# Half a buffer of x's statistics moved to VectorE, the first row's x and k split on VectorE, and the second row's q and k projected before the first row's maxima

## What is computed

```python
# per layer; g(x) is the group norm, C = 32, 8 heads
q = proj(Wq) * C ** -0.5; k = proj(Wk); v = proj(Wv)          # of g(x)
logits = einsum('abhqc,abhkc->abhqk', q, k) + bias (+ mask in layer 1)
weights = softmax(logits, axis=-1)
gate = sigmoid(g(x) @ Wg.T + gating_bias)
x = x + (gate * (weights @ v)) @ Wo.T + bo
```

## Time and profile before

| | us |
|---|---|
| median of 3 runs | 3541.76 (3537.06 to 3541.86) |
| the profiled execution | 3537.66 |
| its span, first to last instruction | 3535.9 |
| first product of the row loop, layer 0 | 111.71 |
| last output products of layer 0 | 1816.19 |
| mean granted TensorE clock | 0.991 |

### The profile page before, as it was taken

How to read it: one execution, slowest core, us unless ns; L and a number is a source line. 1 busy time by engine, 2 the same in 40 slices (tenths; PEclk the granted TensorE clock), 3 DMA queues, 4 the chain that set the end, 5 groups by cost and what they waited for, 6 DMA issues and landing times.

```text
span 3535.9 us, 122483 instructions
## 1 busy us (share of the span) xinstructions
PE 3378.7 (96%) x36216; PEld 2679.8 (76%) x36216; DVE 3392.7 (96%) x11676; ACT 2927.4 (83%) x5457; POOL 3010.4 (85%) x2066
## 2 busy tenths in 40 slices
PE   0799999999999999999979999999999999999997
PEld 0577887778877788777847777877788777887775
DVE  5799999999999999999959999999999999999997
ACT  4588988889888898888857888888888888888885
POOL 3388889888898889888948898898888989898896
PEclk9999999999999999999979999999999999999998
DMA  9555555555555555555545555555555555555552
GB/s 375 166 116 124 125 121 119 118 125 125 119 119 120 125 125 117 119 122 125 120 121 109 120 125 127 124 121 120 126 127 121 120 122 127 127 119 121 123 127 83
DMA packets 463461, 454.11 MB, mean 128 GB/s; under 512 B 55440, under 2 KB 453904, under 8 KB 462880
## 3 DMA queue, kind: packets, MB, share of 16 engines
q1 hardware_dynamic: 255584, 252.91, 29.2%
q10 hardware_dynamic: 207808, 200.33, 26.1%
HBM read 182.39 MB, written 67.24 MB: 71 GB/s over the span
## 4 chain that ended last, share of the span: by engine, by line
PE 93%; DMA 2%; DVE 2%; ACT 1%; SPq 1%; issue 1%; POOL 0%; ACTq 0%; DVEq 0%; POOLq 0%
PE proj_a L922 19%; PE proj_b L922 19%; PE av_bank L949 13%; PE max_bank L933 13%; PE exp_bank L938 12%; PE proj_a L978 10%; PE den_bank L960 6%; PE proj_b L970 1%; DMA probs<-in_xT 1%; DMA k_stack<-k_lo 1%; DVE probs L820 0%; DVE max_bank L808 0%; SPq L376 0%; SPq L306 0%; PE den_bank L908 0%
## 5 line engine op out<-in xcount | busy, mean ns | idle before, releaser
L808 DVE CUSTOM_DVE_ANT_0 max_bank<-max_bank,bias_q 128x256 f32<-128x256 f32 x4096 | 1621.0, 432 | 54.2 <-PE max_bank L933 44.9
L478 POOL TENSOR_TENSOR probs_sum<-probs 128x1024 f32<-128x1024 f32 x508 | 1205.6, 2373 | 356.4 <-ACT probs L519 167.0
L820 DVE TENSOR_TENSOR probs<-exp_bank,bias_k 128x512 f32<-128x512 f32 x2048 | 1378.8, 674 | 10.6 <-PE exp_bank L938 10.6
L933 PE MATMUL max_bank<-k_stack,q_stack 96*128 96x256 f16 (+1 forms) x4096 | 786.5, 273 | 11.5 <-DMA k_stack<-k_lo 8.5
L938 PE MATMUL exp_bank<-q_stack,k_stack 100*128 100x256 f16 x4096 | 784.2, 272 | 9.8 <-DVE probs L820 6.9
L516 ACT ACTIVATE probs<-probs,mask_bias 128x1024 f32<-128x1024 f32 x512 | 560.4, 1142 | 35.2 <-issue 28.4
L519 ACT ACTIVATE probs<-probs 128x1024 f32<-128x1024 f32 x512 | 512.4, 1048 | 39.8 <-issue 33.9
L808 DVE DVE_READ_ACCUMULATOR2_ANT row_max<- 128x1 f32 x4096 | 533.0, 130 | 0.0
L949 PE MATMUL av_bank<-probs,v_sb 128*32 128x256 f32 x8192 | 497.4, 383 | 1.0 <-ACT probs L516 0.6
L938 PEld LDWEIGHTS exp_bank<-q_stack,k_stack 100*128 100x128 f16 x4096 | 394.0, 97 | 74.6 <-DVE probs L820 13.9
L933 PEld LDWEIGHTS max_bank<-k_stack,q_stack 96*128 96x128 f16 (+1 forms) x4096 | 400.7, 99 | 60.8 <-DMA k_stack<-k_lo 9.2
(11 more groups left out here) (171 smaller groups left out, 7038.4 us busy)
## 6 DMA issues: line engine op xcount, KB each, us to landing
q_stack<-q_hi SPq DMA_DIRECT2D x512, 128.0 KB
k_stack<-k_hi SPq DMA_DIRECT2D x512, 128.0 KB
q_stack<-q_lo SPq DMA_DIRECT2D x256, 128.0 KB
k_stack<-k_lo SPq DMA_DIRECT2D x256, 128.0 KB
y<-in_xT ACTq DMA_DIRECT2D x128, 256.0 KB, 3.5
layer_out<-y ACTq DMA_DIRECT2D x128, 256.0 KB, 4.0
y<-layer_out ACTq DMA_DIRECT2D x128, 256.0 KB, 3.6
out<-y ACTq DMA_DIRECT2D x128, 256.0 KB, 3.6
```

Source lines behind the costliest of these rows:

```text
L478: pool.tensor_tensor(probs_sum[:, g], pr[:, :, 0, :], pr[:, :, 1, :], ALU.add).then_inc(sum_ready, 1)
L808: op = dve.tensor_tensor_reduce(out=max_bank[h % 2][:, t, :], in0=max_bank[h % 2][:, t, :], in1=bias_q[:, h, t, :], scale=1.0 / FINE, scal ...
L820: dve.tensor_tensor(probs[:, r.ring(2), h], exp_bank[h % 2][:, :, :], bias_k[:, h], ALU.add).then_inc(logits_ready, 1)
L933: op = pe.matmul(bank_[:, t, :], q[0:n, t * P:(t + 1) * P], k[0:n, :], start=True, stop=True)
```

## The change

Four things are changed.

1. **Statistics.** ScalarE takes only the first 512 tokens of buffer 0 in each turn, VectorE the other 512 of it (two more BN_STATS a turn) and buffers 1 to 3 as before. Buffer 0 is refilled when both have counted it off. `neg_start` comes from VectorE's half of buffer 0.
2. **First row of each layer.** A new function `first_row(l)` on VectorE, between `normalisation(l)` and its slots, makes x_norm, x_hi, x_lo, k_hi and k_lo of row 0. They leave ScalarE (x_norm, x_hi, k_hi, k_f32) and GpSimd (x_lo, k_lo). ScalarE keeps q_hi and q_f32, GpSimd q_lo. ScalarE's table for the exponential is loaded right behind the square root.
3. **Fillers.** In place of 20 behind the group averages and 20 at the end of slot 0: 4 before the first average, 2 between the two, 10 behind them, none in slot 0.
4. **Second row.** In slot 1 of each layer TensorE projects q and k of row 1 at the start, ahead of the first maxima products of row 0, with all waits of these projections; v and gate stay at steps 3 to 5.

The row loop from slot 2 on is unchanged on every engine.

```diff
@@ sync
             def stat_free(c, i):
                 if i == 0:
                     wait(sp, act_stat, 4 * c, sp_passed)
-                else:
-                    wait(sp, stat_used, 3 * c + (i - 3), sp_passed)
+                wait(sp, stat_used, 4 * c + (i - 3), sp_passed)
...
@@ gpsimd, slot
-                    low_half(s, 1)
+                    if not s.first():
+                        low_half(s, 1)
...
                 r = s.plus(1)
-                if r.active():
+                if r.active() and not r.first():
...
@@ scalar
-                    act.activation(out_, x_stat[0][:, ct], ACT.Identity if k < 2 else ACT.Square,
+                    act.activation(out_, x_stat[0][:, ct, 0:512], ACT.Identity if k < 2 else ACT.Square,
...
                 high_gated(s.plus(-5))
-                if s.active():
+                if s.active() and not s.first():
                     split_high(s, 1)
...
@@ vector, statistics
-                    for t in range(n):
-                        op = dve.bn_stats(stats[:, ct, bass.ds(c * (3 * n) + ((i - 1) * n + t), 1), :],
+                    for t in range(1 if i == 0 else 0, n):
+                        op = dve.bn_stats(stats[:, ct, bass.ds(c * STAT_PARTS + (i * n + t - 1), 1), :],
                                           x_stat[i][:, ct, t * 512:(t + 1) * 512])
...
             with dve.Fori(3, STAT_TURNS - 1) as c:
-                for i in range(1, STAT_BUFS):
+                for i in range(STAT_BUFS):
                     statistics(c, i)
...
+            def first_row(l):
+                r = Row(l, 0, 0)
+                i, k_scale = r.ring(2), 1.0 / W_SCALE
...
+                for c in range(CT):
+                    op = dve.tensor_scalar(x_norm[:, i, c], x_in[:, i, c], rstd[:, c:c + 1], shift_x[:, c:c + 1],
+                                           ALU.mult, ALU.add)
+                op.then_inc(x_norm_ready, 1)
...
+                dve.tensor_copy(x_hi[:, i], x_norm[:, i]).then_inc(x_hi_ready, 1)
+                dve.wait_ge(x_hi_ready, r.count(1, 1))
+                dve.tensor_tensor(x_lo[:, i], x_norm[:, i], x_hi[:, i], ALU.subtract).then_inc(x_lo_ready, 1)
+                dve.wait_ge(k_psum, r.count(1, 1))
+                dve.tensor_scalar(qk_hi[1][:, i], pb[:, :, :], k_scale, None, ALU.mult).then_inc(qk_hi_ready[1], 1)
+                dve.wait_ge(qk_hi_ready[1], r.count(1, 1))
+                dve.scalar_tensor_tensor(out=qk_lo[1][:, i], in0=pb[:, :, :], scalar=k_scale, in1=qk_hi[1][:, i],
+                                         op0=ALU.mult, op1=ALU.subtract).then_inc(qk_lo_ready[1], 1)
+                dve.wait_ge(qk_lo_ready[1], r.count(1, 1))
+                dve.sem_inc(qk_f32_ready[1], 1)
...
@@ tensor
+            def project_q(s):
+                wait(pe, v_ready, s.plus(-1).count(1, 1))
+                wait(pe, out_left, s.plus(-6).count(1, 1))
+                pe.wait_ge(x_hi_ready, s.count(1, 1))
+                project(s, 0, pa, 0, None)
+                project(s, 0, pa, 1, q_psum)
+
+            def project_k(s):
+                wait(pe, gate_ready, s.plus(-1).count(1, 1))
+                wait(pe, fine_ready, s.plus(-2).count(1, 1))
+                project(s, 1, pb, 0, None)
+                project(s, 1, pb, 1, k_psum)
+
             def slot(s):
+                second = isinstance(s.turns, int) and s.off == 1
+                if second:
+                    project_q(s)
+                    project_k(s)
...
-                    if step == 7 and isinstance(s.turns, int) and s.off == 0:
-                        keep_busy(20)
...
+                keep_busy(4)
                 pe.wait_ge(norm_v, 6 * l + 1)
                 pe.matmul(pa[:, 0, 0:CT], group_avg[:, :], mean_var[:, :, 0], start=True, stop=True).then_inc(norm_avg, 1)
+                keep_busy(2)
                 pe.wait_ge(norm_c, l + 1)
                 pe.matmul(pb[:, 0, 0:CT], group_avg[:, :], mean_var[:, :, 1], start=True, stop=True).then_inc(norm_avg, 1)
-                keep_busy(20)
+                keep_busy(10)
```

More of the change, by code:

```diff
@@ L76, in active, with first @@
         return not isinstance(self.turns, int) or 0 <= self.off < ROWS
+    def first(self):
+        return isinstance(self.turns, int) and self.off == 0
     def last(self):
@@ L345, in load_bias_k @@
                 else:
[L346 removed]
+                    sp.wait_ge(stat_used, STAT_LOADS)
                     sp.wait_ge(act_stat, 4 * STAT_TURNS)
@@ L567, in slot @@
                     act.dma_start(x_in[:, i], channel_major(src[l], r.index() * TOK, TOK)).then_inc(x_loaded[i], 16)
-                if s.active():
+                if s.active() and not s.first():
                     split_f32(s, 1)
                 r = s.plus(1)
-                if r.active():
+                if r.active() and not r.first():
                     i = r.ring(2)
-                    if r.off == 0 and isinstance(r.turns, int):
+                    if r.off == 1 and isinstance(r.turns, int):
                         act.wait_ge(norm_v, 6 * (l + 1))
@@ L620, in slot @@
                     act.activation(x_hi[:, i], x_norm[:, i], ACT.Copy).then_inc(x_hi_ready, 1)
-                    if r.off == 0 and isinstance(r.turns, int):
-                        act.preload_act_table_set("exp_and_others")
                 if s.active():
@@ L726, in _ @@
             with dve.Fori(3, STAT_TURNS - 1) as c:
-                for i in range(1, STAT_BUFS):
+                for i in range(STAT_BUFS):
                     statistics(c, i)
             c = STAT_TURNS - 1
+            statistics(c, 0)
             statistics(c, 1)
-            dve.wait_ge(stat_used, 3 * c)
-            aggregate(early_mv, 0, 3 * n * c).then_inc(mix, 1)
+            dve.wait_ge(stat_used, 4 * c)
+            aggregate(early_mv, 0, STAT_PARTS * c).then_inc(mix, 1)
             next(mixed)
             statistics(c, 2)
-            tokens = STAT_TURNS * STAT_TOK
+            tokens = STAT_TURNS * 512
             dve.wait_ge(act_stat, 4 * STAT_TURNS)
@@ L996, in slot @@
                         logits(r, h, False)
-                    if step == 1 and s.active():
-                        wait(pe, v_ready, s.plus(-1).count(1, 1))
-                        wait(pe, out_left, s.plus(-6).count(1, 1))
-                        pe.wait_ge(x_hi_ready, s.count(1, 1))
-                        project(s, 0, pa, 0, None)
-                        project(s, 0, pa, 1, q_psum)
-                    if step == 2 and s.active():
-                        wait(pe, gate_ready, s.plus(-1).count(1, 1))
-                        wait(pe, fine_ready, s.plus(-2).count(1, 1))
-                        project(s, 1, pb, 0, None)
-                        project(s, 1, pb, 1, k_psum)
+                    if step == 1 and s.active() and not second:
+                        project_q(s)
+                    if step == 2 and s.active() and not second:
+                        project_k(s)
                     if step == 3 and s.active():
```

38 lines of the change are left out of this document (26 added, 12 removed).

## The result

| | before | after |
|---|---|---|
| median of the runs side by side | 3540.45 (3536.5 to 3545.3, 8 runs) | 3527.68 (3524.64 to 3529.61, 8 runs) |
| the profiled execution | 3537.66 | 3529.61 |
| its span | 3535.9 | 3527.8 |

The ratio is 0.9968, with a 95% interval of 0.9959 to 0.9977: 11.3 us faster (8 to 14.5); the two medians are 12.8 us apart. The forecast was 3525.5 in a range of 3517 to 3535. The two profiled executions differ by 8.1 us only, because that of before was one of the shorter and that of after the longest of eight; hence the means over several profiles further down.

The account below looks back on a forecast made before the run. TensorE and VectorE were taken as 96% busy, leaving only each layer's fill to shorten. Terms 3.7 - 0.4 + 1.2 + 4.0 + 1.2 + 4.3 + 1.0 = 15.0 us, 14.5 kept: 3525.5 us, range 3517 to 3535.

Parts of the forecast that it names:

- N: End of shift_x, closing layer 0's statistics: 3.7 us earlier by the split buffer, less 0.4 for the longer end.
- row 2 to row 3: Interval between these rows' first maxima: no change, VectorE's own work taken to fill each slot behind the third.
- N to first maxima of row 0: First row's split on VectorE with 10 fillers instead of 20: gain 1.2 us in each layer.
- row 0 to row 1: Interval between first maxima with row 1's q and k ahead: 7.7 us, gain 4.0 in layer 0, 4.3 in layer 1.
- row 1 to row 2: Next interval, set by row 2's k_lo: 10.4 us as before in layer 0, 1.0 us gained in layer 1.
- the floor named: Statistics turns: limited by the DMA stream to the shortest turn before, 10.08 us, or 415 GB/s; at most 4.1 us gained.
- the tail: End of the statistics: BN_AGGR over 49 groups in place of 42 costs 0.4 us, all on the path.
- Rival 2: Statistics: the DMA's dry time is not the buffers' doing, so they give nothing; 3527 to 3531 us, chance 0.10.
- The named sign of a wrong step: Start of each layer: first maxima released by TensorE's own q and k instead of by k_lo would show the forecast wrong.
- The join: Before row 0's maxima: row 1's q and k end 7.5 us behind row 0's q, row 0's k_lo lands at 8.3.
- rival 3: Slower: TensorE waits for row 1's inputs ahead of row 0's maxima; whole gain gone at 7.5 us late; chance 0.03.
- Rival 1: Cold start: clock stays low through slots 0 and 1, 4.5 us of a layer's gain lost; 3532 to 3536, chance 0.10.

Follow-up runs that it names:

- l_code: Kernel before with 12 one-column VectorE fills into an unread tile allocated last, no tile moved: 3539.95 us, ratio 1.0006.
- c_order: Kernel before with only q and k of row 1 ahead of row 0's maxima and no fillers in slot 0: 3528.78 us, ratio 0.9974.
- b_nostats: Changed kernel without its statistics part, buffer 0 again ScalarE's alone: 3525.46 us, ratio 0.9966.
- h_both: Changed kernel with 12 fillers ahead of the third row's maxima and VectorE's mask steps moved behind turn 3's first buffer: 3527.16 us, ratio 0.9969.
- e_after: Changed kernel run once more, nothing altered: 3527.10 us, ratio 0.9971 to before.
- n_last: Changed kernel with the statistics tile allocated last and a gap of its old size in its old place: 3524.20 us, ratio 0.9960.
- k_512: Kernel before with an unused tile of 512 bytes a partition behind the statistics: 3535.10 us, ratio 0.9992.
- k_alloc: Kernel before with an unused tile of 384 bytes a partition behind the statistics, no instruction changed: 3543.65 us, ratio 1.0022.
- q_align: p_best with all the rows' tiles 160 bytes further on, the first at a multiple of 512: 3519.16 us, ratio 0.9948.
- p_best: n_last with 12 fillers of 256 columns on TensorE ahead of the third row's maxima: 3521.08 us, ratio 0.9952.

## Why the prediction was right, and where it was not

The table gives the means over all profiles in which a piece is as before, and over all in which it is as changed, with layer 0 and layer 1 where they differ. Each kernel counts with its one profile, layer by layer. l_code is left out of N, and c_order, which has the new order alone, out of row 2 to row 3.

| piece | kernels | as before | as changed | forecast |
|---|---|---|---|---|
| N, layer 0 | 5, 8 | 109.4 | 105.95: -3.4 | -3.7 + 0.4 |
| N to first maxima of row 0 | 6, 8 | 13.43, 12.92 | 11.34, 11.27: -2.1, -1.65 | -1.2, -1.2 |
| row 0 to row 1 | 5, 9 | 11.89, 11.65 | 7.94, 7.75: -3.95, -3.9 | -4.0, -4.3 |
| row 1 to row 2 | 5, 9 | 11.76, 11.19 | 10.47, 10.55: -1.3, -0.6 | 0, -1.0 |
| row 2 to row 3, no fillers there | 5, 4 | 12.70, 12.55 | 13.29, 13.87: +0.6, +1.3 | 0 |
| 29 turns of layer 1 | 7, 6 | 1510.5 | 1513.4: +3.0 | 0 |

The last line compares kernels by where the tiles lie, not by the change's code. The forecast terms add up to -15.0. What was forecast came out at -16.9, 1.9 more than forecast; what was not forecast is +4.9. That leaves -12, against 11.3 (8 to 14.5) measured. That the forecast number was good to 2 us is in part luck: the two misses stood against each other. (The bounds of "8 to 19 us" in the prediction add up, term by term, to some 7.5 and 18.)

**Statistics: right, but not by the floor named.** Forecast -3.3 with the tail. The turns of after took 10.24, 10.65, 10.57, 10.24, 10.22 and 10.00 us, 61.92 together, not six of 10.1: a single shortest turn of before, 10.08, was taken for the typical limit, and the forecast 415 GB/s were 409. In the one pair of profiles the gain is therefore 2.66, less 0.37 for the tail. Over all profiles it is 3.4, since the start of before varies (N 108.46 to 110.27 in five) and the profiled one was early; with the part N lies within 105.57 and 106.23. ScalarE's four passes of 512 columns took 2.8 us (0.70 from one to the next) where 2.6 were taken, which hid as forecast. The tail, +0.4, measured 0.37 (2.42 to 2.81, nothing on the late one). Rival 2 is out.

**First row on VectorE: gained as forecast, but with another wait at its end.** x_norm took 0.74 for the two (forecast 0.54 from the earlier trace rows), x_hi 0.43, x_lo 0.69. q of row 0 ended at N+4.0 where N+3.6 was forecast, and the first maxima are at N+11.80 in after's profile. b_nostats against c_order gives a gain of 1.2 and 1.5 us, where 1.2 and 1.2 were forecast; by the means of the table it is 0.5 to 0.9 more than forecast, because N to the first maxima varies from 12.33 to 14.16 in the kernels before. The named sign of a wrong step did come: the first maxima are released by TensorE's own k of row 1, at 118.06, and not by k_lo, and so in 15 of the 16 places of the eight kernels with this part. The join was forecast with 0.8 us to spare and had none: row 1's x_norm, v and x_hi on ScalarE and x_lo on GpSimd (1.16) put q's fifth matmul at 115.70, 0.32 us late. In layer 1 the fifth matmul waited 0.53 us. So rival 3's mechanism was there, but at its harmless end.

**Row 0 to row 1: right.** 7.7 forecast from VectorE's passes; 7.76 and 7.75 measured, and the same within 0.02 us in all nine kernels with the new order, but for one case in layer 0 of h_both (9.42). Before, it scattered between 10.63 and 12.47; there the granted clock fell to 0.50 at the start of slot 1 in 9 of the 10 places, and the tenth is the one of 10.63. Rival 1 (cold clock in slots 0 and 1) did not come in after: TensorE's matmuls go at the pace of 1.2 GHz (0.22 us for 256 columns) up to about 111 us only. It is not impossible with this change, though: in the one case of h_both the clock was at 0.50 in slot 1, and the slot took 1.67 us more. That is 1 of 18 places.

**Row 1 to row 2: the layers the other way round.** In after's own profile layer 0 lost 0.47 us (k_lo took 4.83 us where the earlier trace rows has 3.95) and layer 1 gained 0.90 of the 1.0. Over the profiles layer 0 gains as well: the 10.41 of before was the shortest of five. The mechanism that the prediction gave for layer 1, a clock at 0.50 in slot 2 that goes with the wait before it, is what both layers show. With the old order TensorE waits 1.51 us for row_max and then 0.53 to 1.86 for k_lo there, in all 10 places, and in 5 of them the clock fell (11.47 to 13.46 us, against 10.41 to 10.97 in the other five). With the new order only the 1.51 is left, and the clock fell in none of 18 (9.80 to 10.99).

**Row 2 to row 3: the step that was missing.** "Behind the third slot VectorE's own work fills each row's slot and the change does not touch it" left out that TensorE's clock can fall there. The wait is the same 1.63 us in before and after, and in every kernel without fillers there. The ten kernels without fillers there have 20 such places. In 9 of them, before's two among them, the clock stayed at 1.00 and the interval is 12.0 or 12.2 us; in 11 it fell to 0.50 for a part of the row and the interval is 13.7 to 13.9, 1.66 us longer. With the new order and the first row on VectorE (after, e_after, n_last, b_nostats) it fell in 7 of 8, in c_order in 1 of 2, with the old order in 3 of 10. In the four kernels with 12 fillers in the gap it fell in none of 8. That the fillers prevent it is shown. Why the same wait lets the clock fall in one execution and not in another is not: the two do not differ in any instruction there, and the wait for k_lo that follows in some does not decide it either (k_512's layer 0, with 0.92 us, fell; k_alloc's layer 1, with 0.88, did not; c_order's layer 0, with none, did). Whether the new order makes the fall more frequent is open with counts this small.

**Layer 1's loop: the other missing step, and it is not in the code's logic.** The prediction gave 0.03 to a loop that moves by 0.02 us a row. Layer 1's moved by 0.027, and not by chance; layer 0's did not move. The larger `stats` tile pushed every tile behind it 384 bytes up. That alone, in k_alloc, makes the DMA engines' packets take 58.2% of the engines' time instead of 55.4, and opens a gap of 0.1 us on TensorE at each turn of layer 1's loop; undone, in n_last, it gives 3 us back. The share follows the remainder: 48.2% at 0, 55.4 at 352 of 512 (96 past a multiple of 256), 58.2 at 224. The Trainium skill (DMA: Bandwidth & Descriptors, How a descriptor splits into AXI transactions) says that a piece that does not start at a multiple of 256 bytes is fetched from the boundary below, and that the bytes before its start still cost beats of 32 bytes. An estimate from that page for a piece of 1,024 bytes, as 396,160 of the packets are: 32 beats at 0, 35 at 96 past, 39 at 224 past, so 9% and 22% more. The order of the three shares agrees, the proportions do not (plus 15% and 21% in the shares), and `y`, which lies at other remainders, is not in the estimate. Where the gap on TensorE comes from is open. It is at the loop's turn, only in layer 1, only where the share is highest, and varies from turn to turn (52.15 to 52.24 us in most) where the turns without it agree within 0.01; that looks like something fetched past busy DMA engines, but the instruction queues moved the same 0.61 and 0.26 MB in both, and no run tests it.

## What to carry to other kernels

Give a new or larger scratch tile a place behind everything that is moved by DMA, or keep the DMA'd tiles at multiples of 512 bytes (256 was not tried): here 384 bytes of scratch took back a fifth of what a change had gained, and 160 bytes of padding made the same transfers take an eighth less of the DMA engines' time. Where TensorE waits some 1.6 us at a join between dense stretches, as here, a dozen filler matmuls that end before the wait does cost nothing and kept its clock each time. And size a term by the range of a row over several executions: the shortest turn, the shortest slot and the start of one profiled run were each taken for typical here.

## What the runs showed of the hardware that was not expected

- The time of identical DMA packets depends on where in SBUF they begin: 48.2, 55.4 and 58.2% of the 16 engines' time for the same 463,392 packets at remainders of 0, 352 and 224 bytes of 512. What that does to the time is less clear: in q_align the wait of 0.59 us for row 2's k_lo, which p_best has, is gone, and the interval is 9.91 us instead of 10.56, but c_order and b_nostats, with tiles at 352, have 9.80 us in the same place without that wait.
- Identical code with one unused tile runs 3 us longer in a loop of 1510 us whose turns otherwise agree within 0.01 us.
- The same wait of 1.63 us on TensorE left the granted clock at 1.00 nine times and was followed by a fall to 0.50 eleven times (0.57 over 4 us in after), at a cost of 1.66 us each.
- The kernel before scatters more than the changed ones: 3531.69 to 3542.08 in 25 runs of one group, against 3524.64 to 3529.61 and 3526.76 to 3527.90 in 8 and 7 runs of the changed one. By the profiles it is N, the way from N to the first maxima, row 0 to row 1 and row 1 to row 2 that scatter in it, the last with the clock's falls in slot 2; row 0 to row 1 is 7.74 to 7.76 us in 17 of 18 places of the new order.
